# One residual block evicted early, scales split, GpSimd's transfer behind the low half, no diagonal

## The reference

```python
x = x + attention(convolution(x))
f = mixed(x)                                   # a small matrix per sample, plus a bias
gate = silu(f @ ((gate_w - gate_z) * gate_s))  # 512 x 1792, scales by groups of 128 rows
up   = f @ ((up_w - up_z) * up_s)
x = x + (gate * up) @ ((down_w - down_z) * down_s)   # 1792 x 512
```

## Time and profile before

| what | value |
|---|---|
| median of 3 runs | 681.24 us (680.61 to 681.83) |
| profiled execution, its own time | 680.94 us |
| its span, first to last instruction | 679.1 us |
| granted TensorE clock, mean | 0.997 of full speed |
| busy: PE, DVE, ACT, POOL | 97%, 83%, 61%, 68% |
| chain that ended last, by engine | PE 75%, DVE 8%, POOL 7%, issue 4%, DMA 3%, ACT 2% |
| GpSimd's accumulating transfers | 24 of 512 KB, 4.6 us to landing in the median |

### The profile page before, as it was taken

The page is one execution under the profiler, slowest core; times in us unless marked ns, Lnnn a source line. Parts: engine busy times, 40 slices in busy tenths (PEclk is TensorE's granted clock), DMA queues, the critical chain, the costliest instruction groups (busy, mean ns, idle before and its releaser), DMA issues.

```text
span 679.1 us, 14435 instructions
## 1 busy us (share of the span) xinstructions
PE 659.5 (97%) x4952; PEld 370.0 (54%) x4952; DVE 563.2 (83%) x870; ACT 411.9 (61%) x1233; POOL 458.5 (68%) x379
## 2 busy tenths in 40 slices
PE   9998999999999999999999999999989999999995
PEld 8855555646566465665656656565644434444441
DVE  4979779879879788987978888777785999899997
ACT  0477663845647384374655638446475778877874
POOL 0367973884685497288659648747537678887886
PEclk9999999999999999999999999999999999999998
DMA  7520157379359348536735943563300156556454
GB/s 262 189 95 1 66 163 140 94 178 183 104 100 270 94 90 268 104 89 158 203 85 106 278 109 77 160 106 102 57 1 0 32 109 124 110 110 139 94 105 113
DMA packets 112672, 82.70 MB, mean 122 GB/s; under 512 B 93264, under 2 KB 93936, under 8 KB 110448
## 3 DMA queue, kind: packets, MB, share of 16 engines
q1 hardware_dynamic: 108736, 69.51, 40.4%
q0 software_dynamic: 3456, 12.58, 9.9%
q10 hardware_dynamic: 432, 0.01, 0.0%
HBM read 48.14 MB, written 2.21 MB: 74 GB/s over the span
## 4 chain that ended last, share of the span: by engine, by line
PE 75%; DVE 8%; POOL 7%; issue 4%; DMA 3%; ACT 2%; SPq 1%; POOLq 0%; DVEq 0%; ACTq 0%
PE bank L677 19%; PE bank L679 18%; PE bank L678 18%; PE bank L1053 2%; PE bank L1054 2%; PE bank L1037 2%; PE bank L1061 2%; PE bank L1038 2%; PE bank L1057 2%; DMA acc<-dprod 2%; POOL wqlo L2156 2%; PE bank L877 1%; DMA wqr<-in_wq 1%; DVE mx L1594 1%; DVE exact L2032 1%
## 5 line engine op out<-in xcount | busy, mean ns | idle before, releaser
L677 PE MATMUL bank<-wohi,oThi 128*128 128x512 f16 x256 | 97.1, 379 | 2.2 <-DVE oTlo L1802 2.1
L677 PE MATMUL bank<-wqhi,cThi 128*128 128x512 f16 x256 | 97.0, 379 | 0.8 <-POOL wqlo L2156 0.6
L678 PE MATMUL bank<-wolo,oThi 128*128 128x512 f16 x256 | 97.0, 379 | 0.0
L679 PE MATMUL bank<-wohi,oTlo 128*128 128x512 f16 x256 | 97.0, 379 | 0.0
L679 PE MATMUL bank<-wqhi,cTlo 128*128 128x512 f16 x256 | 97.0, 379 | 0.0
L678 PE MATMUL bank<-wqlo,cThi 128*128 128x512 f16 x256 | 97.0, 379 | 0.0
L1222 ACT ACTIVATE qraw<-bank 128x512 f32<-128x512 f32 x64 | 37.9, 592 | 82.4 <-PE bank L679 82.1
L2166 POOL TENSOR_TENSOR wolo<-wor,wohi 128x512 f16<-128x512 f32 x32 | 42.6, 1353 | 57.9 <-ACT wohi L1202 57.9
L2204 POOL TENSOR_TENSOR qinv<-qms,neghalf 128x8 f32<-128x8 f32 x28 | 53.6, 1914 | 39.3 <-ACT qms L1241 39.3
L1233 ACT ACTIVATE qsq<-qraw 128x128 f32<-128x128 f32 x256 | 75.5, 302 | 1.7
L677 PE MATMUL bank<-wkvhi,cThi 128*128 128x256 f16 x256 | 69.9, 273 | 0.0
(11 more groups left out here) (231 smaller groups left out, 1806.6 us busy)
## 6 DMA issues: line engine op xcount, KB each, us to landing
acc<-dprod POOLq DMA_DIRECT2D x24, 512.0 KB, 4.6
wqr<-in_wq SPq DMA_DIRECT2D x8, 1024.0 KB, 7.4
wor<-in_wo SPq DMA_DIRECT2D x8, 1024.0 KB, 9.2
raw<-in_gu_w SPq DMA_DIRECT2D x28, 256.0 KB, 3.5
zeros<-in_gu_z SPq DMA_DIRECT2D x28, 256.0 KB, 4.6
wkvr<-in_wkv SPq DMA_DIRECT2D x8, 512.0 KB, 7.2
raw<-in_dn_w SPq DMA_DIRECT2D x14, 256.0 KB, 2.8
zeros<-in_dn_z SPq DMA_DIRECT2D x14, 256.0 KB, 3.5
```

Source lines behind the costliest of these rows:

```text
L677: mm(o, ahi, bhi, start=start and k == 0, stop=False)
L678: mm(o, ahi, blo, start=False, stop=False)
L679: last = mm(o, alo, bhi, start=False, stop=stop and k == n - 1)
```

## The change

1. `turn_x(0, 0)` runs before `gate(1)`, and ScalarE evicts it into `acc` in round 1 (`turned_x(0, 0)`). VectorE's first block of the half is added to it; `result(0)` is gone. In round 16 TensorE transposes c = 1 alone, in round 17 c = 2 and c = 3.
2. The three later scales are written in rounds 8, 13 and 14.
3. `move_down` stands behind `hidden_low` in rounds 3 to 26; in round 27 it stays ahead of `add_part`.
4. `hdiag` is gone; the matmul takes `hrow`, broadcast, against the identity.

```diff
@@ sync
-                sp.wait_ge(d_res, c + 1)
+                if c:
+                    sp.wait_ge(d_res, c)
+                else:
+                    sp.wait_ge(d_dn, down_added(IC - 1, c))
@@ tensor
-                mm(bound_all(), spread[0:MAXIMA, :], hdiag[0:MAXIMA, :], start=True, stop=True).then_inc(t_hx, 1)
+                mm(bound_all(), hrow[0:MAXIMA, :].broadcast_to([MAXIMA, P]), ident[0:MAXIMA, 0:MAXIMA],
+                   start=True, stop=True).then_inc(t_hx, 1)
...
+            turn_x(0, 0)
             gate(1)
             project_out(UNITS - 1, 1, HKV - 1, 1)
             up(1)
+            pe.wait_ge(a_xT, 1)
             project_out(UNITS - 1, 1, HKV - 1, 2)
...
-                elif n in (IC + LAG, IC + LAG + 1):
-                    turn_x(0, 2 * n - 2 * IC - 2 * LAG)
+                elif n == IC + LAG + 1:
+                    turn_x(0, 2)
@@ scalar
-                if i == 0 and g == 0:
-                    act.wait_ge(a_fscl if half else p_fscl, 3 if half else 1)
+                if g == 0 and n in (0, IC):
+                    act.wait_ge(a_fscl if half else p_fscl, 1)
+                elif g == 0 and n == IC + 1:
+                    act.wait_ge(a_fscl, 3)
...
             mix_input(4)
+            turned_x(0, 0)
             scaled(1, 0)
...
-                elif n == IC - 1:
-                    later_scales()
+                elif n in (8, 13, 14):
+                    later_scale((8, 13, 14).index(n))
@@ vector
-                link(V.tensor_reduce(hrow[0:MAXIMA, :], bound_rows(half), AX_X, ALU.max))
-                V.scalar_tensor_tensor(hdiag[0:MAXIMA, :], ident[0:MAXIMA, 0:MAXIMA], TOP,
-                                       hrow[0:MAXIMA, :].broadcast_to([MAXIMA, MAXIMA]), ALU.mult,
-                                       ALU.mult).then_inc(d_hdiag, 1)
+                if half:
+                    dve.wait_ge(t_hx, 2)
+                V.tensor_reduce(hrow[0:MAXIMA, :], bound_rows(half), AX_X, ALU.max).then_inc(d_hrow, 1)
...
-                if n in (IC + LAG, IC + LAG + 1):
-                    result(2 * n - 2 * IC - 2 * LAG)
+                if n == IC + LAG + 1:
+                    result(2)
@@ gpsimd
                 if n > LAG:
                     hidden(n - 1)
+                if n == TILES - 1:
                     move_down(n - 1 - LAG)
                 add_part(n)
                 hidden_low(n - 1)
+                if LAG < n < TILES - 1:
+                    move_down(n - 1 - LAG)
```

More of the change, by code:

```diff
@@ L1004, in hidden_all @@
             def hidden_all(half):
-                pe.wait_ge(d_hdiag, half + 1)
+                pe.wait_ge(d_hrow, half + 1)
                 if half == 0:
                     pe.wait_ge(d_fup, 1)
-                mm(bound_all(), spread[0:MAXIMA, :], hdiag[0:MAXIMA, :], start=True, stop=True).then_inc(t_hx, 1)
+                mm(bound_all(), hrow[0:MAXIMA, :].broadcast_to([MAXIMA, P]), ident[0:MAXIMA, 0:MAXIMA],
+                   start=True, stop=True).then_inc(t_hx, 1)
             def turn_quad(t):
@@ L1114, in turn_x @@
             def turn_x(half, c):
[L1116 to L1119, removed]
+                if half:
+                    pe.wait_ge(a_xT, c + 1)
+                    if c == 0:
+                        pe.wait_ge(d_y, HQ * UNITS)
+                        pe.wait_ge(a_hm, 2)
                 elif c:
-                    pe.wait_ge(a_xT, c)
-                else:
-                    pe.wait_ge(d_y, HQ * UNITS)
-                    pe.wait_ge(a_hm, 2)
+                    pe.wait_ge(a_xT, 1 + KC)
+                    if c > 1:
+                        pe.wait_ge(d_res, c - 1)
+                else:
+                    pe.wait_ge(a_hm, 1)
                 for t in range(HQ):
@@ L1447, in gate, with later_scale @@
                 A(whole[:, n % 2, :], whole[:, n % 2, :], ACT.Silu).then_inc(a_silu, 1)
-            def later_scales():
-                act.wait_ge(p_fdown, 2)
+            def later_scale(k):
                 act.wait_ge(l_gus, 16)
-                A(uscl[:, 1, :, :], gus[:, 1, :, :], ACT.Copy, scale=fdown[:, 1:2]).then_inc(a_fscl, 1)
-                A(gscl[:, 1, :, :], gus[:, 0, :, :], ACT.Copy, scale=finv[:, 1:2]).then_inc(a_fscl, 1)
-                A(dsc[:, 1, :, :], dscl[:, :, :], ACT.Copy, scale=hdown[:, 1:2]).then_inc(a_fscl, 1)
+                if k == 0:
+                    act.wait_ge(d_fup, 2)
+                    A(gscl[:, 1, :, :], gus[:, 0, :, :], ACT.Copy, scale=finv[:, 1:2]).then_inc(a_fscl, 1)
+                elif k == 1:
+                    act.wait_ge(p_fdown, 2)
+                    A(uscl[:, 1, :, :], gus[:, 1, :, :], ACT.Copy, scale=fdown[:, 1:2]).then_inc(a_fscl, 1)
+                else:
+                    act.wait_ge(d_hup, 2)
+                    A(dsc[:, 1, :, :], dscl[:, :, :], ACT.Copy, scale=hdown[:, 1:2]).then_inc(a_fscl, 1)
             def hidden_scale(half):
@@ L1464, in up_first @@
                     act.wait_ge(p_fscl, 2)
+                elif n == IC:
+                    act.wait_ge(a_fscl, 2)
                 if n >= 2:
@@ L1484, in down_scaled, with turned_x @@
                   scale=dsc[:, half, i, c:c + 1]).then_inc(a_dn, 1)
-            def turned_x(c):
-                act.wait_ge(t_xT, c + 1)
-                A(acc[:, 1, place(c), :], side[:, :], ACT.Copy).then_inc(a_xT, 1)
+            def turned_x(half, c):
+                act.wait_ge(t_xT, half + c + 1)
+                A(acc[:, half, place(c), :], side[:, :], ACT.Copy).then_inc(a_xT, 1)
             mix_out(1)
@@ L1988, in hidden_bound, with hidden_maxima @@
                 V.tensor_reduce(hx[:, 0:1], fmx[:, half, 0:HQ], AX_X, ALU.max).then_inc(d_hx, 1)
[L1990 removed]
+            def hidden_maxima(half):
                 dve.wait_ge(t_hx, 2 * half + 1)
[L1992 to L1995 removed]
+                if half:
+                    dve.wait_ge(t_hx, 2)
+                V.tensor_reduce(hrow[0:MAXIMA, :], bound_rows(half), AX_X, ALU.max).then_inc(d_hrow, 1)
             def hidden_power(half):
@@ L2045, in down_added_to @@
                 if n == IC:
-                    dve.wait_ge(a_xT, c + 1)
-                if n:
+                    dve.wait_ge(a_xT, c + 2)
+                elif n == 0 and c == 0:
+                    dve.wait_ge(a_xT, 1)
+                if n or c == 0:
                     if c == 3 and n == DIRECT:
```

13 lines of the change are left out of this document (6 added, 7 removed).

## The result

The change takes **685.07 us** (median of 14 runs, 682.68 to 688.93) where the kernel before takes 681.63 us in the same sessions (14 runs): ratio **1.0045**, 95% interval 1.0023 to 1.0066. (The ratios on record are not the quotients of the medians shown; here those give 1.0050.) It is slower, by 0.45% where 0.3% was forecast, and inside the stated range. The profiled execution took 685.03 us, with a span of 683.2 us instead of 679.1.

What follows compares the result with a forecast made beforehand. TensorE, called busy for 97% of the span, was taken as the bound, with a short list of stalls. Terms -1.85 + 0.2 - 0.1 - 0.85 + 2.5 + 2.1 = +2.0 gave a median of 683.2 us, range 681.3 to 685.8.

Steps and rivals of the forecast that it cites:

- the two places: Round 17 and the tail, where later transfers were to make engines wait: +2.5 and +2.1 us.
- The half boundary: TensorE's stalls at 593.22 and before 594.88 go with the transfer behind the low half: 1.3 and 0.35 us.
- Round 9: A held GpSimd issue makes TensorE's start at 569.79 come 0.2 us late; moving the transfer removes that.
- The transposes of the second half: The second half's first gate product may wait for its input's transposes: +0.2 us, bounds none to 1.9.
- The diagonal: Dropping VectorE's 4x4 operation per half gains 0.1 us in the first half and 0.85 in the second.
- The block and the scales: Early residual block in round 1, scales in rounds 8, 13 and 14: 0 us, covered by other waits.
- Round 17: VectorE waits for transfer 13, landing at 612.6, and TensorE's transposes wait behind it: +2.5 us, bounds 2.3 to 3.0.
- The clock: TensorE's clock was to stay at 2.4 GHz in the new waits; a rival at 0.20 had it fall.
- The likeliest case: The forecast itself, chance 0.58: median 683.2 us, with no fall of the clock.
- a clock under 1.0 before the last matmul: Listed sign that the prediction is wrong: TensorE's granted clock below 1.0 before its last matmul.
- The tail: Round 27: transfer 24 waits for the later transfer 23, delaying the last sum and final additions: +2.1 us, bounds 1.9 to 2.5.
- the rival of the clock: The clock falls in the new wait of round 17, costing 2.5 us more: 685.7 us, chance 0.20.

Runs made afterwards that it cites:

- run 4: The kernel before with only GpSimd's transfer moved behind the low half, in all rounds but the last: 688.42 us, ratio 1.0106.
- run 2: The change with result 2 where result 1 stood, and result 1 computed later: 681.91 us, ratio 1.0008.
- Run 7: run 3 with the last rows of the second half's input prepared in round 10 instead of 11: 679.12 us, ratio 0.9951.
- run 6: The kernel before without the diagonal and nothing else changed: 680.38 us, ratio 0.9974.
- run 5: The kernel before with only the early residual block and the scales in three: 681.70 us, ratio 0.9994.
- run 12: The change plus twelve unread TensorE products in round 17, before the transposes that wait for result 1: 683.50 us, ratio 1.0022.
- run 3: run 2 with GpSimd's transfer in front again from round 17 on and a separate semaphore for the second half: 679.85 us, ratio 0.9977.
- run 8: run 3 with one semaphore, so round 17's transfer waits for transfer 13's landing: 680.62 us, ratio 0.9985.
- run 11: The kernel before without the diagonal, transfers in front, last rows prepared in round 10 instead of 11: 679.53 us, ratio 0.9970.
- run 10: run 3 with the results in the change's order, so result 1 waits for transfer 13: 683.67 us, ratio 1.0028.

## Why the prediction was right, and where its sizes were off

The side, the two places and the order of the costs were right. The profiled execution was 4.1 us longer where the sum said 2.0. By its steps:

- **The half boundary.** -1.3 and -0.35 forecast, -1.32 and -0.36 measured.
- **Round 9.** -0.2 forecast. The stand before 569.79 went (0.23 us), but the three small products that now lie behind the issue cost 0.30 in the same round (run 4's third price). The forecast had no term for them.
- **The transposes of the second half.** This term was mis-sized: +0.2 taken, +0.51 measured (and a TensorE stand of 1.5 us in run 2). The argument was that the traffic is unchanged; what changed is who is last. The transfer is issued 2 us later, and the last of the transposes, issued 0.51 us behind it, lands 0.40 behind it, at 590.07. Before the change the last one landed at 590.12: the transposes did not move with the rest. Run 7 took the wait away.
- **The diagonal.** -0.95 forecast in the two halves, -1.05 measured, and 1.1 us in run 6. That all of the 0.92 us of that row goes, and not 0.16, was the right choice: beside a multiplication of the same length (1.70 us) the reduction took 0.27 and the product 0.73 us, and neither waited for its end.
- **The block and the scales.** 0 forecast, 0.9994 (0.9980 to 1.0007) in run 5. The cover named for the scales was there.
- **Round 17.** The mechanism stood as written: issue behind the low half, landing after its reader, VectorE, then TensorE. +2.5 forecast, +2.66 measured. Even the times stood: the kernel was 1.84 us ahead when round 16 began, and with that put back the issue of 606.24 is at 608.1 (608.0 forecast), the landing at 612.6 (612.6), and the transposes are at 613.6 (613.45). The other 0.43 is the block's, as in the sum.
- **The clock.** The forecast held that it would not fall, and gave 0.20 to the rival in which it does. It fell, in both traces of the change and by the mean clocks not in all executions, and run 12 shows that idleness was the reason. The rival had 2.5 us for it, taken from the start of the kernel; it was 1.47 us, of which 0.51 or less was absorbed later. That reading of the start was loose: the matmuls of L731 only begin at 4.66 us, so 6 against 20 of them tells no pace, and the profile puts a granted clock of 1.00 on both stretches. The halved pace is in the busy time of one, 0.22 us against 0.11. The likeliest case was the wrong one of the two: the result lies 0.6 us from the rival's 685.7 and 1.9 us from the forecast's 683.2, and "a clock under 1.0 before the last matmul", a sign of being wrong, came true.
- **The tail.** +2.1 forecast, +2.74 measured. The chain was the one described: transfer 23 late, 24 waits for it with the last sum behind, then the gapless additions. The excess comes from transfer 22, which took 5.3 us to land; the forecast had no late landing there. With the lag of 1.35 put back, 23 went at 663.2, not 662.5. With the transfers in front from round 17 on the last one went 3.9 us sooner than in run 2 and the kernel took 2 us less (run 3); with one chain instead of two it went 3.7 sooner and took 1.6 less by the ratios (run 8).

So the forecast was 2.1 us short: 1.0 from the clock, 0.6 in the tail, 0.3 at the transposes, 0.3 in round 9, the rest small. The direction rests on the mechanism. That the size lies inside the range does not: the range reached up to 685.8 only for the rival of the clock.

The change's gain did not vanish by being hidden: 1.7 us at the boundary and 1.05 at the diagonal are in the trace. It was paid back, at the two places where a reader of the last landing exists. Whether the placement can pay at all is not settled. Moved only as far as round 16, with the reader moved too and the second half on a chain of its own, the kernel is as fast (run 3, 0.9977) as the one before without its diagonal (run 6, 0.9974). With the last rows earlier as well, it is run 7 (0.9951) against run 11 (0.9970): 1.3 us by the ratios, 0.4 by the medians, with intervals that overlap. The 2.4 us by which run 7 beats the kernel before are thus for 1.1 the diagonal's, and the rest is not parted.

## What to carry to other kernels

When an issue is moved later, list the readers of its landing, the one after the last transfer above all, and move them with it. A chain of transfers whose period (issue to next issue, 5.1 us here) is hardly shorter than the loop's (5.2 us) makes up only 0.1 us of a delay in a round: put the issue in front again where nothing reads the landing late. Where its target changes, a new semaphore spares one stand, for likely 0.5 us. Give a stand of TensorE such as those of 2.2 to 3.0 us here a rival price of up to its own length again for the clock (2.98 us in run 10 were followed by some 6 us at half pace), and fill it if it can't be removed.

## What was not expected of the hardware

- The clock behind a stand is not a matter of the stand's length alone: 2.73 us in run 4 left it at 1.00, 2.18 us in the same run brought it to 0.51, and 2.88, 2.87 and 2.98 us brought it to 0.53, 0.57 and 0.52, for 3.3 us twice and 6.2 us once. In runs 4 and 6 it was at half from 499.8 to 503.2 us as well, where TensorE had been idle for at most 0.88 us at a time, but often; in the kernel before, with the same gaps, it was not. Why is open.
- A transfer of 512 KB lands 4.5 to 5.0 us after its issue when at most 150 packets of others and none of the `instruction` kind fall into it (153 transfers in the 14 traces). Beside 800 and more packets of transposes, and no `instruction` packet, it took 4.9 to 5.6 (10 transfers). With an `instruction` packet of q8 between 0.7 and 4.2 us after its issue it took 4.9 to 6.5 (14 transfers); with one earlier, or between 4.2 and 4.5 us, 4.5 to 4.6; with one after that 4.7 to 6.9, but a packet so late meets only a transfer that is not quick. The packet falls now into one round, now into another. In the kernel before it fell into transfer 9, beside 1106 packets of transposes: the late landing (6.5 us) is the stand at the half boundary that the change set out to remove. That the packet is the cause was not tested by itself, only seen.
- A transpose of SyncE that is issued while GpSimd's transfer is under way landed behind it in every trace, mostly 0.2 to 0.6 us behind if issued in its first 2 us, and up to 7.1 us after its own issue (run 6), where the fastest took 2.3.
